# A retention and FP4 feed-forward kernel: the transposes of the normalised heads go behind the value projection, the gate projection ahead of the output projection

## The chip, the cores and the metric

The kernel runs on one core of a Trainium2 chip. The metric is the device time of one execution in microseconds; a comparison is between medians of runs. The granted clock that the profile gives for TensorE (PE) is a share of full speed, where 1.00 is 2.4 GHz and 0.50 is 1.2 GHz.

## The reference

Two sequences of 2048 tokens with 256 features each pass through a retention layer and a feed-forward layer, each with a residual and a layer norm:

```
q, k, v = split(x @ w_qkv.T);  q, k = xpos(q, k)          # 8 heads, 32 wide; v 64 wide
ret = einsum(q, k) * scale * decay ** (t - s)  (causal)
o   = einsum(ret, v);  normed = (o - mean(o)) / sqrt(var(o) + EPS)   # per head
x   = layernorm(x + (silu(x @ w_gated.T) * normed) @ w_proj.T)
xq, wq = fp4_quant_dequant(x), fp4_quant_dequant(w)       # blocks of 16
x   = layernorm(x + fp4_linear(silu(gate) * up, w_down))
```

## The kernel before

The 4096 tokens are 32 tiles of 128 tokens; the tiles alternate between the two sequences, so a tile's state depends on that of the tile two before. Tile n is worked on in "body n". Every engine has its own hand-written `body(n, b, piece)`, with b = n % 2, and runs its instructions in that order; semaphores tie the engines together. Bodies 8 to 29 are in a hardware loop over pairs of tiles; those before and behind are written out. The feed-forward stage (`ffn_body`) follows for all tiles. Most products are made of three float32r products (high by high, high by low, low by high), so each needs a high and a low copy of its input.

TensorE's body n before the change, in order (n+1 is the next tile, n-3 an older one, since `LAG` is 3):

1. `turn_qk(n)` (L1396): four transposes of the rotated queries and keys into the PSUM bank `turn`.
2. `project_qk(n+1)` (L1362), a product of six 512-column matmuls.
3. `scores(n)` (L1410), which waits for ScalarE's `copy_qkT(n)` (L433) and `open_gate(n)` (L443), and for VectorE's `add_resid` (L681) of tile n-4.
4. `turn_gated(n-3)` (L1459): four transposes of the gated, normalised heads into `turn`. It waits for `gated_ready` of tile n-3 and for VectorE's `decay_q(n)` (L666), which reads the same bank.
5. `update(n)` (L1446) and `cross(n)` (L1421), the new state's product and the product with the carried state; `cross` waits for `decay_q(n)`.
6. `project_v(n+1)` (L1362). It writes `proj[:, 1]`, one of the four banks in which the scores lie, and so waits for `ret_ready` of tile n: VectorE's `decay_scores(n)` (L674), which reads all the scores.
7. `mix(n)` (L1433), the product of the decayed scores and the values.
8. `project_out(n-3)` (L1362 on `wproj`), twelve 256-column matmuls, which waits for VectorE's `split_gated(n-3)` (L1078); its result goes to `add_resid(n-3)`, `resid_stats` and `resid_moments`.
9. `project_gate(n+1)` (L1362), which waits for `ret_ready` too.

ScalarE starts its body with `copy_qkT(n)` and then `open_gate(n)`; further down come `copy_gatedT(n-3)` (L413, out of `turn`), `place_state` (L477), `copy_v(n+1)` (L438) and `square_heads(n)` (L448). VectorE has `decay_q`, `decay_scores`, short steps of the quantisers and of the inverse square roots, `split_gated`, then `rotate_products` and `rotate_sum` (L647 to L659) of tile n+1, on which the next `turn_qk` waits; then `apply_gate` (L691), `add_resid`, `resid_stats`, `sum_squares` (L698), and in even bodies `x_max` (L781). Bodies 0 to 2 have no `turn_gated` and no `project_out`, because there is no tile n-3. In body 31 there is no tile n+1, and weight transposes of the feed-forward layer (`turn_weights`) stand ahead of and behind `mix`.

Of the kernel before, what the change touches and what calls it, by code (L numbers as in the profile page):

```python
# [35 lines left out]
TILES = BATCH * CHUNKS  # L36
# [37 lines left out]
LAG = 3  # L74
# [16 lines left out]
def retention_ffn(nc, x_tok, x_feat, w_in, w_proj, w_gu, w_down, decay, tables, eye, pow_dram, out):  # L91
    with ExitStack() as ctx:
# [196 lines left out]
        def in_turn(n):  # L289

            return valid(n) and valid(n + LAG)
# [108 lines left out]
        def _(act):  # L400
# [9 lines left out]
            def copy_gatedT(n):  # L410
                act.wait_ge(gated_turned, n + 1)
                need(act, y_done, n)
                act.activation(gatedT_hi[:], turn[:], ACT.Copy).then_inc(gatedT_ready, 1)  # L413
# [6 lines left out]
            def round_w_from(piece):  # L420
                act.wait_ge(w_fp4["step"], FP4_STEPS * (piece + 1))
                part = w_fp4["rounder"][:, 0]
                act.activation(part, part, ACT.Copy, bias=ROUNDER_FROM, scale=ROUNDER_BY).then_inc(w_fp4["rounder_ready"], 1)
# [56 lines left out]
            def body(n, b, piece):  # L480
                if valid(n):
                    copy_qkT(n)
                if valid(n):
                    open_gate(n, b)
                if valid(n + 2) and not (isinstance(n, int) and n < 0):
                    split_x(n + 2, b)
                low, high = range(PER), range(PER, HEADS)
                if valid(n - 2) and b == 1:
                    normalise_half(n - 2, b, low)
                if in_turn(n - LAG):  # L490
                    copy_gatedT(n - LAG)
                if valid(n - 2) and b == 1 and not weights(n, 0):
                    normalise_half(n - 2, b, high)
                if piece is not None and b == 1:
                    round_w_from(piece)
                for group in weights(n, 0):
                    turn_weights(group)
                if carried(n - 1):
                    place_state(n - 1, 1 - b)
                if valid(n + 1):  # L500
                    copy_v(n + 1, 1 - b)
                if isinstance(n, int) and n == 0:
                    act.wait_ge(ld_proj, 32)
                    act.activation(wproj_hi[:], wproj, ACT.Copy).then_inc(wproj_hi_ready, 1)
                if valid(n - 2) and b == 0:
                    normalise_half(n - 2, b, low)
                if valid(n):
                    square_heads(n)
                if valid(n - 2) and b == 0:
                    normalise_half(n - 2, b, high)  # L510
                if b == 1 and tiles_of(n - 1) and not (isinstance(n, int) and n == TILES - 1):
                    round_x_from(n - 1)
                for group in weights(n, 1):
                    turn_weights(group)
                if weights(n, 1):
                    split_xq(0, 0)
                    normalise_half(n - 2, b, high)
                if b == 0 and tiles_of(n):
                    norm_x1(n)
# [102 lines left out]
        def _(dve):  # L622
# [38 lines left out]
            def decay_q(n):  # L661
                dve.wait_ge(qkT_ready, n + 1)
                if isinstance(n, int) and n == 0:
                    dve.wait_ge(ld_dq, 16 * PER)
                need(dve, out_done, n)
                dve.tensor_tensor(qdT[:].rearrange("p g t -> p (g t)"), turn[:, 0:GROUPS * P],  # L666
                                  dq[:].rearrange("p g t -> p (g t)"), ALU.mult).then_inc(qd_ready, 1)

# [23 lines left out]
                                  gate[:, b].rearrange("p (g r c) -> p r g c", g=GROUPS, r=2), ALU.mult).then_inc(opened_ready, 1)  # L692

            def sum_squares(n, b):
                need(dve, resid_stats_done, n - LAG + 1)
                need(dve, joint_ready, n - b)
                dve.wait_ge(squared, n + 1)
                dve.tensor_reduce(moments[:, b, 2:2 + HEADS], head_cols(squares[:]), AX.X, ALU.add).then_inc(heads_summed, 1)  # L698
# [159 lines left out]

            def body(n, b, piece):
                joint, x, w = b == 0 and valid(n - 2), b == 1 and bool(tiles_of(n - 1)), piece is not None  # L860
                if joint:
                    joint_var(n)
                    joint_guess(n)
                if valid(n):
                    decay_q(n)
                if valid(n):
                    decay_scores(n)
                if x:
# [12 lines left out]
                if w and b == 1:  # L881
                    w_unit(piece)
                    w_exponent(piece)
                if in_turn(n - LAG):
                    split_gated(n - LAG)
                if joint:
                    joint_fine(n)
                for group in weights(n, 0):
# [7 lines left out]
                if x and not (isinstance(n, int) and n == TILES - 1):  # L896
                    x_unit(n - 1)
                    x_exponent(n - 1)
                if valid(n + 1):
                    rotate_products(n + 1, 1 - b)  # L900
                    rotate_sum(n + 1, 1 - b)
# [5 lines left out]
                    turn_weights(group)  # L907
                if weights(n, 1):
                    split_xq(0, 0)
                if in_turn(n - LAG):  # L910
                    add_resid(n - LAG, 1 - b)
                    resid_stats(n - LAG, 1 - b)
                if valid(n):
                    sum_squares(n, b)
                if in_turn(n - LAG):
                    resid_moments(n - LAG, b)
                if b == 0 and tiles_of(n):
                    x_max(n)
                if isinstance(n, int) and n == -1:
# [307 lines left out]

            def finish(n):
                if n == 0:
                    joint_chain(TILES)  # L1230
                    split_gated(TILES - LAG)

# [125 lines left out]
        def _(pe):  # L1358
# [115 lines left out]
            def body(n, b, piece):  # L1474
                if valid(n):
                    turn_qk(n, b)
                if valid(n + 1):
                    project_qk(n + 1, 1 - b)
                if valid(n):
                    scores(n)  # L1480
                if in_turn(n - LAG):
                    turn_gated(n - LAG, 1 - b)
                if carried(n):
                    update(n, b)
                if valid(n):
                    cross(n, b)
                for group in weights(n, 0):
                    turn_weights(group)
                if valid(n + 1):
                    project_v(n + 1, 1 - b)  # L1490
                if isinstance(n, int) and n == -1:
                    flip_mask()
                if valid(n):
                    mix(n, b)
                for group in weights(n, 1):
                    turn_weights(group)
                if isinstance(n, int) and n == TILES - 1:
                    turn_xq(0, 0)
                if in_turn(n - LAG):
                    project_out(n - LAG)  # L1500
                if valid(n + 1):
                    project_gate(n + 1, 1 - b)

            def flip_mask():

# [136 lines left out]
```

## Time and profile before

| what | us |
|---|---|
| median of 3 runs | 589.22 |
| lowest, highest | 589.04, 592.42 |
| the profiled execution | 590.8 |
| its span | 589.0 |
| TensorE busy in it | 565.3 |
| VectorE busy in it | 513.6 |

TensorE's matmul ends are modelled, so its busy time hides short waits. Starts are measured: the distance from the start of one group of weight loads (PEld) to the next says how long a step of TensorE lasted, waiting included. "issue" behind a row names idle time for which the trace has no releaser.

### The profile page before, as it was taken

To read this page: it belongs to the slowest core of one execution; us is meant where nothing else is said; L and a number is where in the kernel's file an instruction comes from. 1 tells how busy PE (TensorE), PEld (TensorE's weight loads), DVE (VectorE), ACT (ScalarE), POOL (GpSimd) and SP (SyncE) were. 2 spreads that over 40 slices of the span, in tenths; PEclk is the share of its full clock that TensorE was granted. 3 is DMA by queue.
4 is the path that set the end of the run, shared out by engine and by line. 5 is a ranking of instruction groups with operands and counts; after the bars stand their busy time and mean duration, and the time that the engine had idled before them with its cause. 6 is when DMAs were issued, how large, how long until landed. Compare 5 with 4: busy or idle time off the path is not lost.

```text
span 589.0 us, 14053 instructions
## 1 busy us (share of the span) xinstructions
PE 565.3 (96%) x4432; PEld 486.4 (83%) x4432; DVE 513.6 (87%) x1283; ACT 338.0 (57%) x818; POOL 228.3 (39%) x260
## 2 busy tenths in 40 slices
PE   6999999999999999999999879999999999999983
PEld 3778888888888888888888768889999999999973
DVE  6567878988998998899899858999999999888896
ACT  3446766766676676667667634435444545445442
POOL 2211121435334343533434213554655645554420
PEclk9999999999999999999999979999999999999997
DMA  6601210210111011001101000000010101000002
GB/s 206 219 20 46 55 46 12 55 53 18 36 53 45 9 53 53 26 28 53 45 9 45 11 9 11 0 1 2 1 37 1 37 1 37 18 20 19 19 18 90
DMA packets 24983, 22.32 MB, mean 38 GB/s; under 512 B 2025, under 2 KB 21874, under 8 KB 24946
## 3 DMA queue, kind: packets, MB, share of 16 engines
q1 hardware_dynamic: 24130, 20.27, 11.6%
q10 hardware_dynamic: 816, 1.57, 0.9%
q8 instruction: 21, 0.34, 0.3%
q14 instruction: 16, 0.13, 0.1%
HBM read 17.63 MB, written 4.20 MB: 37 GB/s over the span
## 4 chain that ended last, share of the span: by engine, by line
PE 86%; DVE 7%; DMA 2%; issue 2%; POOL 2%; ACT 1%; ACTq 0%; DVEq 0%; POOLq 0%
PE wide_banks L1362 58%; PE wide_banks L1433 9%; PE wide_banks L1410 4%; PE wide_banks L1421 3%; PE wide_banks L1550 3%; PE turn L1459 3%; PE turn L1396 2%; PE wide_banks L1446 2%; DVE shared L852 1%; DVE shared L857 1%; DVE shared L674 1%; PE turn L1559 1%; DMA pow_dram<-powers 1%; DMA wgu_lo<-pow_dram 1%; POOL shared L1323 1%
## 5 line engine op out<-in xcount | busy, mean ns | idle before, releaser
L1328 POOL TENSOR_TENSOR shared<-shared,h_scale 128x704 f32<-128x704 bf16 x31 | 43.0, 1388 | 78.7 <-DVE shared L857 78.7
L1362 PE MATMUL wide_banks<-win_hi,x_hi 128*128 128x512 f32 x192 | 66.5, 428 | 2.6 <-DVE shared L674 1.5
L461 ACT ACTIVATE shared<-opened,rstd 128x64 f32<-128x64 f32 x240 | 63.6, 340 | 2.2 <-DVE rstd L770 2.1
L1433 PEld LDWEIGHTS wide_banks<-shared 128*128 128x128 f32 x512 | 62.0, 192 | 2.8
L1362 PE MATMUL wide_banks<-wgu_hi,xq_hi 128*128 128x512 f32 (+1 forms) x192 | 60.7, 397 | 3.4 <-DVE xq_lo L1065 3.4
L556 ACT ACTIVATE shared<-wide_banks 128x512 f32<-128x512 f32 x64 | 29.6, 462 | 58.0 <-PE wide_banks L1362 57.5
L1433 PE MATMUL wide_banks<-shared 128*128 128x64 f32 x512 | 60.6, 271 | 0.0
L1362 PE MATMUL wide_banks<-win_hi,x_lo 128*128 128x512 f32 x192 | 60.4, 396 | 0.0
L1362 PE MATMUL wide_banks<-win_lo,x_hi 128*128 128x512 f32 x192 | 60.3, 395 | 0.0
L1362 PE MATMUL wide_banks<-wgu_lo,xq_hi 128*128 128x512 f32 (+1 forms) x192 | 57.4, 380 | 0.0
L1362 PE MATMUL wide_banks<-wgu_hi,xq_lo 128*128 128x512 f32 (+1 forms) x192 | 57.0, 379 | 0.0
L427 ACT ACTIVATE shared<-shared 128x704 bf16<-128x704 f32 x32 | 25.3, 791 | 54.0 <-POOL shared L1323 51.6
L1323 POOL TENSOR_TENSOR shared<-shared,h_inv 128x704 f32<-128x704 f32 x31 | 43.2, 1392 | 26.7 <-DVE h_inv L848 26.7
L674 DVE TENSOR_TENSOR shared<-wide_banks,shared 128x1024 f32<-128x1024 f32 x32 | 39.2, 1225 | 14.4 <-PE wide_banks L1410 14.4
L1279 POOL TENSOR_TENSOR x_lo<-xf,x_hi 128x256 fp32r<-128x256 f32 x32 | 23.3, 728 | 70.9 <-DVE qdT L666 42.9
L433 ACT ACTIVATE qkT<-turn 128x512 f32<-128x512 f32 x32 | 19.2, 599 | 42.9 <-PE turn L1396 42.9
L1362 PEld LDWEIGHTS wide_banks<-win_hi,x_lo 128*128 128x128 f32 x192 | 36.1, 188 | 8.7
L1362 PEld LDWEIGHTS wide_banks<-win_lo,x_hi 128*128 128x128 f32 x192 | 36.2, 189 | 8.2
L1362 PEld LDWEIGHTS wide_banks<-wgu_hi,xq_lo 128*128 128x128 f32 x192 | 36.1, 191 | 6.1
L1362 PEld LDWEIGHTS wide_banks<-wgu_lo,xq_hi 128*128 128x128 f32 x192 | 36.1, 191 | 6.0
L1269 POOL TENSOR_TENSOR x_unit<-x_unit,x_rounder 128x512 f32<-128x512 f32 (+1 forms) x17 | 20.8, 1225 | 50.7 <-DVE shift L775 46.8
L1245 POOL TENSOR_TENSOR kd<-shared 128x128 f32<-128x128 f32 x60 | 23.2, 407 | 38.6 <-DVE shared L659 34.4
(146 smaller groups left out, 1438.9 us busy)
## 6 DMA issues: line engine op xcount, KB each, us to landing
xf<-in_x_feat SPq DMA_DIRECT2D x32, 128.0 KB, 2.2
tab<-in_tables SPq DMA_DIRECT2D x16, 256.0 KB, 2.7
xt<-in_x_tok SPq DMA_DIRECT2D x32, 128.0 KB, 2.1
out<-x SPq DMA_DIRECT2D x32, 128.0 KB, 1.7
x<-in_w_in ACTq DMA_DIRECT2D x3, 512.0 KB, 5.8
w<-in_w_gu SPq DMA_DIRECT2D x1, 1408.0 KB, 8.0
w<-in_w_down SPq DMA_DIRECT2D x1, 704.0 KB, 9.3
wgu_lo<-pow_dram SPq DMA_DIRECT2D x1, 576.0 KB, 4.5
```

What stands on the lines that cost most here:

```text
L427: act.activation(h_size[:, b], h_unit[:, b], ACT.Abs, scale=SIZE_BY).then_inc(h_fp4["rounder_ready"], 1)
L461: last = act.activation(gated[:, b, cols], opened[:, b, cols], ACT.Copy, scale=rstd[:, b, 1 + k:2 + k])
L556: act.activation(silu[:, cols[0]:cols[1]], proj[:, part, 0:cols[1] - cols[0]], ACT.Silu).then_inc(silu_done[part], 1)
L674: dve.tensor_tensor(ret[:].rearrange("p (j g) t -> p j (g t)", g=GROUPS), row_scores, dmask[:].rearrange("p (j g) t -> p j (g t)", g=GROUP ...
L1245: last = pool.tensor_tensor(kd[:, P * g:P * (g + 1)].rearrange("p (j d) -> p j d", d=DQ), rot[:, b, QK + P * g:QK + P * (g + 1)].rearrange ...
L1269: pool.tensor_tensor(unit, unit, rounder, ALU.add).then_inc(x_fp4["rounded"], 2)
L1279: pool.tensor_tensor(x_lo[:, b], xf[:, b], x_hi[:, b].bitcast(F32), ALU.subtract).then_inc(x_lo_ready, 1)
L1323: pool.tensor_tensor(over_blocks(h_unit[:, b]), over_blocks(h[:, b]), spread(h_fp4["inv"][:]), ALU.mult).then_inc(h_fp4["step"], 1)
L1328: pool.tensor_tensor(over_blocks(hq[:, b]), over_blocks(h_steps[:, b]), spread(h_fp4["scale"][:, b]), ALU.mult).then_inc(h_fp4["ready"], 1)
L1362: last = pe.matmul(dst, lhs, rhs, start=k == 0, stop=k == len(parts) - 1)
L1410: last = pe.matmul(row_scores[:, j, P * g:P * (g + 1)], qkT[rows, GROUPS + g], qkT[rows, g], start=True, stop=True)
L1433: last = pe.matmul(mixed[:, r, DV * at:DV * (at + 1)], ret[:, slot(k)], vs[:, b, DV * k:DV * (k + 1)], start=False, stop=k >= HEADS - 2, s ...
```

## The change

TensorE: `turn_gated(n-3)` goes from behind `scores(n)` to behind `project_v(n+1)`, directly ahead of `mix(n)`; `project_gate(n+1)` goes ahead of `project_out(n-3)`. ScalarE: `copy_gatedT` goes behind `copy_v`, `round_w_from` behind that. VectorE: `decay_q` opens the body; `resid_moments` goes from the end of a body into the next one, behind `decay_q`; `split_gated` goes behind `x_unit` and `x_exponent`, directly ahead of `rotate_products`; `sum_squares` goes ahead of `add_resid`. A wait of `sum_squares` on the residual's statistics goes to `decay_q`, for a tile one older. The last `resid_moments` is in `finish(0)`.

```diff
 # TensorE
                 if valid(n):
                     scores(n)
-                if in_turn(n - LAG):
-                    turn_gated(n - LAG, 1 - b)
                 if carried(n):
                     update(n, b)
 ...
                     project_v(n + 1, 1 - b)
                 if isinstance(n, int) and n == -1:
                     flip_mask()
+                if in_turn(n - LAG):
+                    turn_gated(n - LAG, 1 - b)
                 if valid(n):
                     mix(n, b)
 ...
+                if valid(n + 1):
+                    project_gate(n + 1, 1 - b)
                 if in_turn(n - LAG):
                     project_out(n - LAG)
-                if valid(n + 1):
-                    project_gate(n + 1, 1 - b)
 # ScalarE
-                if in_turn(n - LAG):
-                    copy_gatedT(n - LAG)
 ...
-                if piece is not None and b == 1:
-                    round_w_from(piece)
 ...
                     copy_v(n + 1, 1 - b)
+                if in_turn(n - LAG):
+                    copy_gatedT(n - LAG)
 ...
+                if piece is not None and b == 1:
+                    round_w_from(piece)
 # VectorE
+                need(dve, resid_stats_done, n - LAG)          # in decay_q
 ...
-                need(dve, resid_stats_done, n - LAG + 1)      # in sum_squares
 ...
+                if valid(n):
+                    decay_q(n)
+                if valid(n) and valid(n - 1 - LAG):
+                    resid_moments(n - 1 - LAG, 1 - b)
                 if joint:
                     joint_var(n)
                     joint_guess(n)
-                if valid(n):
-                    decay_q(n)
 ...
-                if in_turn(n - LAG):
-                    split_gated(n - LAG)
 ...
+                if in_turn(n - LAG):
+                    split_gated(n - LAG)
                 if valid(n + 1):
                     rotate_products(n + 1, 1 - b)
 ...
+                if valid(n):
+                    sum_squares(n, b)
                 if in_turn(n - LAG):
                     add_resid(n - LAG, 1 - b)
                     resid_stats(n - LAG, 1 - b)
-                if valid(n):
-                    sum_squares(n, b)
-                if in_turn(n - LAG):
-                    resid_moments(n - LAG, b)
 # VectorE, finish(0)
+                    dve.wait_ge(resid_stats_done, TILES - LAG)
+                    resid_moments(TILES - 1 - LAG, 1)
```

## Rows read from the trace of the kernel before

**Rows 1.** Page: TensorE's busy time, and its granted clock in 40 slices.
```profile
PE 565.3 (96%) x4432; PEld 486.4 (83%) x4432; DVE 513.6 (87%) x1283; ACT 338.0 (57%) x818; POOL 228.3 (39%) x260
...
PEclk9999999999999999999999979999999999999997
```

**Rows 2.** Timeline (start, us, engine, line, what), one looped tile: TensorE's weight loads.
```profile
200.16 0.54 PEld L1410 LDWEIGHTS wide_banks<-qkT 32*128 32x128 f32 x16 [0.36 <-issue]
...
200.82 0.42 PEld L1459 LDWEIGHTS turn<-ident,shared 128*128 128x128 f32 x4
...
201.41 0.27 PEld L1446 LDWEIGHTS wide_banks<-shared,kd 128*32 128x32 f32 x16 [0.17 <-issue]
...
201.77 0.52 PEld L1421 LDWEIGHTS wide_banks<-shared,qdT 64*128 64x128 f32 x8
...
202.41 0.30 PEld L1362 LDWEIGHTS wide_banks<-win_hi,x_hi 128*128 128x128 f32 x2
...
203.69 1.98 PEld L1433 LDWEIGHTS wide_banks<-shared 128*128 128x128 f32 x16
...
205.59 0.54 PEld L1362 LDWEIGHTS wide_banks<-wproj_hi,gatedT_hi 128*128 128x128 f32 x4
...
207.01 0.31 PEld L1362 LDWEIGHTS wide_banks<-win_hi,x_hi 128*128 128x128 f32 x2
...
208.28 0.59 PEld L1396 LDWEIGHTS turn<-ident,shared 128*128 128x128 f32 x4
...
210.45 0.54 PEld L1410 LDWEIGHTS wide_banks<-qkT 32*128 32x128 f32 x16 [0.37 <-issue]
```

**Rows 3.** Timeline, the same tile: what VectorE and ScalarE do around the scores.
```profile
200.96 1.23 DVE L674 TENSOR_TENSOR shared<-wide_banks,shared 128x1024 f32<-128x1024 f32 x1 [0.25 <-PE wide_banks L1410]
...
209.16 0.60 ACT L433 ACTIVATE qkT<-turn 128x512 f32<-128x512 f32 x1 [0.76 <-PE turn L1396]
...
209.65 0.59 ACT L443 ACTIVATE shared<-wide_banks 128x512 f32<-128x512 f32 x1
```

**Rows 4.** Timeline, tile 2, which has no turned heads and no output product.
```profile
37.05 0.57 PEld L1410 LDWEIGHTS wide_banks<-qkT 32*128 32x128 f32 x16 [0.38 <-issue]
...
37.74 0.27 PEld L1446 LDWEIGHTS wide_banks<-shared,kd 128*32 128x32 f32 x16
37.87 1.23 DVE L674 TENSOR_TENSOR shared<-wide_banks,shared 128x1024 f32<-128x1024 f32 x1 [1.07 <-PE wide_banks L1410]
38.10 0.52 PEld L1421 LDWEIGHTS wide_banks<-shared,qdT 64*128 64x128 f32 x8
...
39.21 0.30 PEld L1362 LDWEIGHTS wide_banks<-win_hi,x_hi 128*128 128x128 f32 x2 [0.58 <-issue]
...
39.24 0.70 PE L1362 MATMUL wide_banks<-win_hi,x_hi 128*128 128x512 f32 x2 [0.42 <-DVE shared L674]
...
40.48 1.99 PEld L1433 LDWEIGHTS wide_banks<-shared 128*128 128x128 f32 x16
...
45.84 0.56 PEld L1410 LDWEIGHTS wide_banks<-qkT 32*128 32x128 f32 x16 [0.38 <-issue]
```

**Rows 5.** Timeline, the looped tile again: ScalarE's and VectorE's rows near the moved steps.
```profile
204.11 0.60 ACT L438 ACTIVATE shared<-wide_banks 128x512 f32<-128x512 f32 x1 [0.78 <-PE wide_banks L1362]
...
205.24 0.69 DVE L647 TENSOR_TENSOR qk_cos<-wide_banks,tab 128x512 f32<-128x512 f32 x1
...
206.97 0.41 DVE L659 TENSOR_TENSOR shared<-qk_cos,wide_banks 128x256 f32<-128x256 f32 x1
...
210.54 0.41 DVE L666 TENSOR_TENSOR qdT<-turn,dq 128x256 f32<-128x256 f32 x1
```

**Rows 6.** Timeline at the change of stages, and busy time by stretch (PE, PEld, DVE, ACT, POOL, PEclk, DMA, GB/s).
```profile
345.08 1.22 PE L1362 MATMUL wide_banks<-wgu_hi,xq_hi 128*128 128x512 f32 x2 [3.20 <-DVE xq_lo L1065]
...
345.00:350.00 5.00, 4.92 (x14) 3.97 (x15) 4.39 (x16) 1.19 (x2) 1.25 (x2) 0.50 0.09 26
```

## The prediction

> **What bounds the kernel now.** I read the page first. TensorE is busy for 565.3 of 589.0 us, at a granted clock of nine tenths or more in all slices but two [rows 1]. Busy time of TensorE can't show a short wait, so I went to the timeline and took the distances between the starts of its groups of weight loads. In the loop one tile takes 210.45 - 200.16 = 10.29 us [rows 2] (all 26 distances from tile 4 to tile 30 are 10.28 to 10.30), made up so: scores 0.66, turned heads 0.59, state product 0.36, cross product 0.64, value projection 1.28, mix 1.90, output product 1.42, gate projection 1.27, and 2.17 from the start of `turn_qk` to the next scores [rows 2].
>
> Two links in this chain go over another engine. The first is that last 2.17 us: transposes, ScalarE's copy of them (209.16 to 209.76) and its gate (to 210.24), then scores at 210.45, 0.21 behind the gate's end [rows 2, 3]. The query and key projection in between is six 512-column matmuls, 1.28 us like its sister, and 2.17 - 0.57 (the transposes) - 1.28 leaves about 0.3 us of waiting. The second runs from scores over VectorE's `decay_scores` to `project_v`: the decay starts 0.80 us behind the scores' start and takes 1.23 [rows 3], so it ends at 202.19, and the value projection starts at 202.41 [rows 2]. TensorE's own work between the two, 0.66 + 0.59 + 0.36 + 0.64 = 2.25 us, just covers this link. The turned heads are 0.59 of that cover.
>
> **What the cover is worth: tiles 0 to 2.** Bodies 0 to 2 have no turned heads, so they already have TensorE's order of the changed kernel between scores and `project_v`. In tile 2 [rows 4] the scores start at 37.05, the state product follows 0.69 later, the cross product at 1.05, and the value projection at 39.21, which is 2.16 behind the scores. Its weight load has 0.58 us of idle time ahead of it and its first matmul 0.42 us, put down to `decay_scores`, which ran from 37.87 to 39.10. Tiles 0 and 1 show the same 2.14 and 2.16. So the link over VectorE takes 2.16 us with nothing but 1.7 us of work inside it, and 2.25 us with the turned heads inside: the four transposes cost 2.25 - 2.16 = 0.09 us where they stand.
>
> **The change part by part.**
>
> *Turned heads behind `project_v`.* In the new place nothing waits beside them: the engine runs value projection, transposes, mix in sequence. Their price there is a transpose group between full products. `turn_qk`, the same four transposes, takes 0.57 us in such a place, 0.59 in the old one with its 0.17 of issue [rows 2]. So each tile gives back 0.09 and pays 0.57: +0.48, or +0.50 with 0.59. A gain is excluded by the 2.16 of rows 4, unless `decay_scores` itself gets shorter or starts earlier, and it starts 0.80 (before) and 0.82 (tile 2) behind the scores, released by TensorE both times [rows 3, 4]. The least it can cost is 0, if the 0.58 of idle time in tiles 0 to 2 had a cause of its own; the most is 0.59 + 0.09 = 0.68, if the transposes also break up the pipelining of their new neighbours as much as they gain now. I take 0.50.
>
> *Gate projection ahead of the output product.* Both keep their 1.27 and 1.42 us [rows 2]. Could the gate now be opened earlier, which would shorten the 0.3 us wait ahead of scores? ScalarE still has `copy_qkT` ahead of `open_gate` in its queue, and starts it only at 209.16 when the transposes are done; the gate projection had ended before that even in the old order [rows 2, 3]. So 0. The swap hides the heads' new path: transposes at 3.43 behind the scores (2.16 + 1.27), ScalarE's copy behind `copy_v`. `copy_v` starts 1.70 behind its projection's start (202.41 to 204.11) [rows 2, 5], so at 3.86, and the copy of the heads ends at about 3.86 + 0.5 + 0.6 = 4.96; VectorE's `split_gated` ends near 5.7. Mix starts at 4.00, gate at 5.90, output product at 7.17: 1.5 us of slack. Without the swap it would be 0.2.
>
> *VectorE's order.* `split_gated` now stands directly ahead of the rotations. In even bodies they start at 5.08 now [rows 5] (205.24 - 200.16) and at about 5.65 then, and the rotated keys are ready near 7.8 rather than 7.22 (207.38). The next `turn_qk` stands at 7.17 + 1.42 = 8.59, so 0.6 us is left after the 0.2 of a release. Behind them: amax of a weight piece, gate, squares' sum, residual (near 9.4 to 9.8; scores at 10.79 waits for it), statistics, `x_max`, and `decay_q` of the next body at about 10.83, which is 0.05 behind the next scores; now it is at 0.09 (210.54 to 210.45) [rows 2, 5]. Then `resid_moments`, and VectorE is free for `decay_scores` about 0.6 behind the scores, with 0.80 wanted. The cover there is 0.2 us, in every second tile. `cross` waits for `decay_q`, ends 0.45 behind the scores, wanted at 1.02. I cost all of this at 0. GpSimd, which gets the rotated keys about 0.6 us later, has till the next state product, 0.66 behind the next scores, so 3.6 us for 0.8 of work.
>
> **Sum.** New period: 2.16 + 1.27 + 0.58 + 1.90 + 1.27 + 1.42 + 2.17 = 10.77 to 10.79. It can be checked from the other side: tile 2's period is 8.79 [rows 4], and with output product and transposes added it is 8.79 + 1.42 + 0.57 = 10.78. From scores 3 to scores 31 are 28 periods, 28 x 0.50 = 14.0. In body 31 weight transposes take `project_v`'s place and wait for the same decay; the turned heads come behind them and push all that follows by 0.59. 14.0 + 0.6 = 14.6 us. The span becomes 589.0 + 14.6 = 603.6, the profiled execution 590.8 + 14.6 = 605.4, and the median 589.22 + 14.6 = 603.8.
>
> *The clock.* In tiles 0 to 2 TensorE waits 0.42 us in the matmul row of each tile, and slices 2 and 3 of the page, from 14.7 us on, stand at nine tenths or more [rows 1, 4]. So waits of 0.5 us per tile left the clock at its full level. The Trainium skill, "Perfetto Trace Analysis", section Matmul Optimizations, says that the matmul engine scales its power with its use and that matmuls should therefore run back to back. That rule speaks against this change; the trace, with 0.42 us per tile at the full clock, doesn't show it for waits of this size. By the rule the sum would be more than 14.6; by the rows it is 14.6.
>
> **Rivals.**
>
> A. *The transposes are free in the new place (not slower).* Place: the start of `project_v`. If the 0.58 us of idle time in tiles 0 to 2 came from something that the loop doesn't have, `project_v` would follow the cross product at 0.66 + 0.36 + 0.64 = 1.66, and the 0.59 taken away there would pay for the 0.59 added: 589.2 us. It decides from the point at which `decay_scores` ends less than 1.5 us behind the scores' start. Against it: its end at 2.03 in both rows [rows 3, 4]. 5%.
>
> B. *The gate comes early.* If the wait ahead of scores hung on the gate projection and not on ScalarE's order, up to 0.33 us per tile would go: 29 x 0.33 = 9.6, so 603.8 - 9.6 = 594.2. Against it: ScalarE's gate starts directly behind the copy [rows 3]. 4%.
>
> C. *VectorE becomes late for `decay_scores`.* If its row in even bodies is 0.5 us longer than I count, the 0.2 of cover is gone and each second tile loses 0.3: 14 x 0.3 = 4.2, so 608.0. For it: VectorE's row from the rotations on has no gap. 13%.
>
> D. *The half clock at the change of stages.* Behind a 3.20 us wait of TensorE the clock stands at 0.50 in 345 to 350 [rows 6]; with its edges (0.91 in the 5 us on either side) it is some 6.8 us at half speed, which cost about 3.1 us of the work that ran in it from 345.08 on. If this doesn't happen in the changed kernel, 603.8 - 3.1 = 600.7; if it happens once more, 606.9. For it: one of three runs before was 3.2 us longer. 13%.
>
> E. *Half clock in the loop,* the rule above. If the clock fell for such a stretch once in the stage, it would be 606.9, and if in every other tile, 14 x 3.1 = 43 us more, 647. Against it: rows 1 and 4. 1%.
>
> **Numbers.** The forecast itself has 64%: 603.8 us, with its own bounds 0.40 and 0.60 per tile, so 601 to 607. C and both halves of D lie inside 599.5 to 608.5, A, B and E's far end outside, and that leaves out no more than 2 in 10 with the outer parts of C and D. A difference of over 1% (5.9 us) is about what a measurement of this kernel tells from no change. Slower by over 1%: the forecast, C, D and E, 0.90 after a share for what I don't see. Within 1%: A and B, 0.07. Faster: 0.03, since no rival worked out here reaches it.
>
> **What would show it.** Right, if the looped period is 10.78 us; `project_v` starts 2.15 to 2.17 behind scores, with an idle time of about 0.58 before its weights and 0.42 before its matmul, put down to L674, in all tiles; the transposes (L1459) take 0.57 between `project_v` and mix; scores still follow ScalarE's gate by 0.2. Wrong, if `project_v` starts at 1.7 (A), if scores start less than 2.1 behind `turn_qk` (B), or if L674 starts later than 0.8 behind the scores in every second tile (C).

## The result, and the profile after

| | median of runs, us | runs | ratio to before, 95% interval |
|---|---|---|---|
| before | 590.17 | 4 | |
| after | 603.00 (601.25 to 605.43) | 4 | 1.0214 (1.0185 to 1.0244) |

The change makes the kernel about 12.8 us slower. The profiled execution of after has a span of 601.9 us, 12.9 more than before's. It splits so, by the start of the scores of tile 3 and of tile 31: up to tile 3 1.45 us (45.84 to 47.29), the 28 periods from tile 3 to tile 31 10.77 us (287.86 to 298.63), and what follows 0.68 us (255.30 to 255.98).

The page of after (busy time; TensorE's clock in 40 slices):

```profile
PE 566.8 (94%) x4432; PEld 490.2 (81%) x4432; DVE 515.9 (86%) x1283; ACT 336.0 (56%) x818; POOL 228.3 (38%) x260
...
PEclk9999999999999999999999989999999999999998
```

TensorE's busy time has grown by 1.5 us against [rows 1]; all the rest of the 12.9 is new idle time. The waits of after's TensorE (us in total, times, longest):

```profile
PE wide_banks L1364 <- DVE shared L675: 14.7, 31, 0.8
```

L675 is `decay_scores`, L1364 the wide product. Before had four such waits, 1.5 us in all. One looped tile of after in the timeline, from its `turn_qk` (tile 19, an odd one), to be laid beside [rows 2, 4]:

```profile
215.90 0.47 PEld L1398 LDWEIGHTS turn<-ident,shared 128*128 128x128 f32 x4
216.00 0.60 PE L1398 MATMUL turn<-ident,shared 128*128 128x128 f32 x4
...
217.93 0.54 PEld L1412 LDWEIGHTS wide_banks<-qkT 32*128 32x128 f32 x16 [0.36 <-issue]
217.93 0.73 PE L1412 MATMUL wide_banks<-qkT 32*128 32x128 f32 x16
...
218.59 0.27 PEld L1448 LDWEIGHTS wide_banks<-shared,kd 128*32 128x32 f32 x16
...
218.72 1.22 DVE L675 TENSOR_TENSOR shared<-wide_banks,shared 128x1024 f32<-128x1024 f32 x1 [0.25 <-PE wide_banks L1412]
218.95 0.52 PEld L1423 LDWEIGHTS wide_banks<-shared,qdT 64*128 64x128 f32 x8
...
220.06 0.30 PEld L1364 LDWEIGHTS wide_banks<-win_hi,x_hi 128*128 128x128 f32 x2 [0.59 <-issue]
220.09 0.70 PE L1364 MATMUL wide_banks<-win_hi,x_hi 128*128 128x512 f32 x2 [0.43 <-DVE shared L675]
...
221.34 0.60 PEld L1461 LDWEIGHTS turn<-ident,shared 128*128 128x128 f32 x4
...
221.57 0.60 PE L1461 MATMUL turn<-ident,shared 128*128 128x128 f32 x4
...
221.90 1.87 PEld L1435 LDWEIGHTS wide_banks<-shared 128*128 128x128 f32 x16
222.01 1.90 PE L1435 MATMUL wide_banks<-shared 128*128 128x64 f32 x16
...
223.69 0.30 PEld L1364 LDWEIGHTS wide_banks<-win_hi,x_hi 128*128 128x128 f32 x2
223.72 0.72 PE L1364 MATMUL wide_banks<-win_hi,x_hi 128*128 128x512 f32 x2
...
224.97 0.66 PEld L1364 LDWEIGHTS wide_banks<-wproj_hi,gatedT_hi 128*128 128x128 f32 x4
```

The 0.43 us of idle time ahead of the value projection is tile 2's picture of [rows 4], now in every tile. The slots, from start to start of weight loads, in us:

| slot | before [rows 2] | after | difference |
|---|---|---|---|
| scores to value projection | 2.25 | 2.13 | -0.12 |
| value projection | 1.28 | 1.28 | 0 |
| turned heads in the new place | | 0.56 | +0.56 |
| mix | 1.90 | 1.79 | -0.11 |
| gate projection | 1.27 | 1.28 | +0.01 |
| output product | 1.42 | 1.56 | +0.14 |
| `turn_qk` to scores | 2.17 | 2.03 | -0.14 |
| one tile | 10.29 | 10.63 | +0.34 |

Odd tiles of the loop take 10.63 us, even ones 10.72; the mean over tiles 9 to 28 is 10.68 against 10.28.

Four of these differences (0.56, -0.11, 0.14, -0.14) are partly a matter of where the ruler is laid. The first weight load of a group starts some way ahead of its first matmul, and this lead differs: the transposes' load stands 0.23 us ahead behind 512-column matmuls (221.34 to 221.57) and 0.10 ahead behind 256-column ones (215.90 to 216.00), that of mix 0.11 ahead behind the transposes. From the start of one group's matmuls to the next, the turned heads take 222.01 - 221.57 = 0.44 us and mix 1.71, as in before (1.70). From `turn_qk` to the scores it is 217.93 - 216.00 = 1.93 us, and in before 1.93 too:

```profile
208.52 0.60 PE L1396 MATMUL turn<-ident,shared 128*128 128x128 f32 x4
...
210.45 0.73 PE L1410 MATMUL wide_banks<-qkT 32*128 32x128 f32 x16
```

### The profile page after: what moved, and what is told of

Read it like the earlier page. It is cut to its first block and busy times, and to the rows that moved or that the text cites. A ratio compares the mean times of both kernels' runs of the same rounds, so it can differ in the third digit from the quotient of the medians.

```text
span 601.9 us, 14053 instructions
## 1 busy us (share of the span) xinstructions
PE 566.8 (94%) x4432; PEld 490.2 (81%) x4432; DVE 515.9 (86%) x1283; ACT 336.0 (56%) x818; POOL 228.3 (38%) x260
## 5 line engine op out<-in xcount | busy, mean ns | idle before, releaser
L1364 PE MATMUL wide_banks<-win_hi,x_hi 128*128 128x512 f32 x192 | 68.8, 439 | 14.9 <-DVE shared L675 14.7
L1364 PE MATMUL wide_banks<-wgu_hi,xq_hi 128*128 128x512 f32 (+1 forms) x192 | 60.2, 395 | 3.4 <-DVE xq_lo L1065 3.4
L461 ACT ACTIVATE shared<-opened,rstd 128x64 f32<-128x64 f32 x240 | 62.1, 340 | 0.4
L556 ACT ACTIVATE shared<-wide_banks 128x512 f32<-128x512 f32 x64 | 29.6, 462 | 57.0 <-PE wide_banks L1364 56.5
L1435 PEld LDWEIGHTS wide_banks<-shared 128*128 128x128 f32 x512 | 60.6, 194 | 0.3
L1364 PE MATMUL wide_banks<-win_lo,x_hi 128*128 128x512 f32 x192 | 60.4, 396 | 0.0
L1364 PE MATMUL wide_banks<-win_hi,x_lo 128*128 128x512 f32 x192 | 60.3, 395 | 0.0
L1364 PE MATMUL wide_banks<-wgu_lo,xq_hi 128*128 128x512 f32 (+1 forms) x192 | 57.0, 378 | 0.0
L1364 PE MATMUL wide_banks<-wgu_hi,xq_lo 128*128 128x512 f32 (+1 forms) x192 | 56.8, 377 | 0.0
L438 ACT ACTIVATE shared<-wide_banks 128x512 f32<-128x512 f32 x32 | 19.1, 597 | 58.3 <-PE wide_banks L1364 58.3
L675 DVE TENSOR_TENSOR shared<-wide_banks,shared 128x1024 f32<-128x1024 f32 x32 | 39.0, 1220 | 9.3 <-PE wide_banks L1412 9.3
L1364 PEld LDWEIGHTS wide_banks<-win_hi,x_hi 128*128 128x128 f32 x192 | 29.2, 191 | 21.8 <-issue 21.7
L1364 PEld LDWEIGHTS wide_banks<-win_hi,x_lo 128*128 128x128 f32 x192 | 36.1, 188 | 8.7
L1364 PEld LDWEIGHTS wide_banks<-win_lo,x_hi 128*128 128x128 f32 x192 | 36.1, 188 | 8.7
L1364 PEld LDWEIGHTS wide_banks<-wgu_hi,xq_lo 128*128 128x128 f32 x192 | 35.8, 189 | 6.0
```

Source lines behind the costliest of these rows:

```text
L438: act.activation(vs[:, b], proj[:, 1], ACT.Copy).then_inc(v_copied, 1)
L461: last = act.activation(gated[:, b, cols], opened[:, b, cols], ACT.Copy, scale=rstd[:, b, 1 + k:2 + k])
L556: act.activation(silu[:, cols[0]:cols[1]], proj[:, part, 0:cols[1] - cols[0]], ACT.Silu).then_inc(silu_done[part], 1)
L675: dve.tensor_tensor(ret[:].rearrange("p (j g) t -> p j (g t)", g=GROUPS), row_scores, dmask[:].rearrange("p (j g) t -> p j (g t)", g=GROUP ...
L1364: last = pe.matmul(dst, lhs, rhs, start=k == 0, stop=k == len(parts) - 1)
L1435: last = pe.matmul(mixed[:, r, DV * at:DV * (at + 1)], ret[:, slot(k)], vs[:, b, DV * k:DV * (k + 1)], start=False, stop=k >= HEADS - 2, s ...
```

## Experiments

Theory 1: the four transposes were TensorE's cover for the way from the scores over VectorE's `decay_scores` to the value projection, and cost their own time in the new place. Theory 2: the loss comes from the new orders of VectorE and ScalarE, or from the swap of the two products. Periods below are those of the loop in the profiled run of each kernel.

**The decay in two parts.** The value projection overwrites one of the four banks that the decay reads. This kernel is after, with that bank decayed first and the value projection waiting for it alone (the code is shortened).

```diff
+ for rows, done in ((slice(0, 1), ret0_ready), (slice(1, PER), ret_ready)):
+     dve.tensor_tensor(ret[rows], row_scores[:, rows], dmask[rows], ALU.mult).then_inc(done, 1)
 # project_v
-                need(pe, ret_ready, n)
+                need(pe, ret0_ready, n)
```

> The changed kernel with decay_scores cut in two: the bank that project_v overwrites first (a quarter of the columns), then the other three; project_v waits for the first alone. Theory 1: first part about 0.4 us, so it ends near 1.2 behind scores' start, and project_v starts at 1.66 to 1.7 (behind cross, no wait), not at 2.14: period 10.67 - 0.47 = about 10.2 us, and the time falls by 12 to 13 us to about that of the kernel before. Theory 2: only the extra instruction on VectorE is seen, 0.1 to 0.2 us a tile, and the time stays at after's or above (+13 to +18 against before).

586.15 us, ratio to before 0.9944 (0.9913 to 0.9975), some 2.6% below after by the two ratios. Its timeline, tile 19:

```profile
207.65 0.54 PEld L1414 LDWEIGHTS wide_banks<-qkT 32*128 32x128 f32 x16 [0.36 <-issue]
...
208.45 1.29 DVE L677 TENSOR_TENSOR shared<-wide_banks,shared 128x256 f32<-128x256 f32 x2 [0.24 <-PE wide_banks L1414]
208.67 0.52 PEld L1425 LDWEIGHTS wide_banks<-shared,qdT 64*128 64x128 f32 x8
...
209.31 0.30 PEld L1366 LDWEIGHTS wide_banks<-win_hi,x_hi 128*128 128x128 f32 x2
```

The value projection starts 1.66 us behind the scores, with no idle time, and odd tiles take 10.15 us, 0.48 less than in after. Both numbers are those that theory 1 gave. Even tiles take 10.28, because the decay starts later there (see `joint_guess` below). The 28 periods are 13.4 us shorter than in after, as expected; the time fell by some 16 us (by the two ratios) and not by 12 to 13. Tiles 0 to 2 won another 1.4 us (8.30 to 8.33 each, from 8.76 to 8.80), and in the profiled run the clock stood at 1.00 from 330 to 360 us, behind the loop, where after's and before's fell for a while. Taking away this one wait gives back more than the whole loss, with all new orders in place.

**The same cut in the kernel before.** The same edit as above, on before.

> The kernel before with the decay cut in two as in the changed one. Theory 1: the way over VectorE is just covered there by TensorE's 2.25 us, so the cut can give at most the small rest: project_v at 2.25 still, period 10.28 (10.17 at best, as for a wait of 0.1 us), time 0 to 3 us below before; that it gives 15 us in the changed kernel and next to none here is what shows that the turned heads were the cover. Rival: if it gives 10 us or more here too, the cut helps in another way and the split run says nothing about the change.

588.68 us, 0.9985 (0.9972 to 0.9998): 0.9 us at the most likely. The value projection stays at 2.25 behind the scores in odd tiles, the period at 10.28; even tiles are 10.32 to 10.36, and only tiles 0 to 2, which have no turned heads, go from 8.77 to 8.79 down to 8.32 to 8.39. Where the transposes stand in the way the loop has nothing to win; where they are gone the same cut is worth 2.7% of before's time, some 16 us.

**Three of four transposes left out, in before and in after; and all four done twice, in after.** Each of the three ran once, so they are read by their periods.

```diff
-                for c in range(VC):                 # turn_gated, tiles 0 to 28
+                for c in range(1):                  # left out
+                for c in list(range(VC)) * 2:       # twice
```

> The kernel before with only the first of the four transposes of the gated heads in tiles 0 to 28; three are left out, as in the other run. Cover theory: their room between scores and project_v is nearly free, since project_v can't start before 2.14 to 2.16 behind scores anyway: project_v moves from 2.25 to 2.14, the period from 10.28 to 10.17, 3 us in all, with an idle time of 0.2 to 0.3 us ahead of it. Rival: if transposes cost TensorE their own time in either place, the period falls by 0.33 here too, 9 us in all.

> The changed kernel with only the first of the four transposes of the gated heads in the loop's tiles (0 to 28); the other three are left out, so three quarters of the turned heads are wrong there. Price of a transpose in the new place: TensorE's clean rate would be 0.11 us each, so the turned heads' slot shrinks by 0.33 us and so does the period: 10.63 to 10.30 in odd tiles, 9 to 10 us less in all. If the new place were free (rival A): no change of the period.

> The changed kernel with the four transposes done twice in tiles 0 to 28 (the result is the same). Four more at the clean rate of 0.11 us: 0.44 to 0.47 us per tile, period 11.07 to 11.10 in odd tiles, 12 to 13 us more than after. If the prediction's 0.57 for four transposes was right and only something else made after's period shorter: 0.57 per tile, 16 us more.

Before's period falls to 10.16 to 10.21, most often 10.17 or 10.18, so about 0.11 us for three transposes. Its span is 584.5, 4.5 less, of which 2.85 are in the 28 periods. The value projection now starts at 2.14 with idle time ahead of it:

```profile
210.75 0.30 PEld L1362 LDWEIGHTS wide_banks<-win_hi,x_hi 128*128 128x128 f32 x2 [0.34 <-issue]
```

In after the odd period falls to 10.31, so 0.32 us for the same three. The even one falls only from 10.72 to 10.52, by 0.20: `decay_scores` starts 1.02 us behind the scores there, and the value projection 2.34. The 28 periods are 7.6 us shorter, the span is 592.9, 9.0 less. Twice four raise the odd period to 11.07 and the even one to 11.16, by 0.44 each, the 28 periods by 12.3 us and the span to 613.2, 11.3 more. A transpose in the new place costs 0.11 us, four cost 0.44. With 0.57 for four, as predicted, the last run would have had 11.20. Here are its matmuls: eight transposes from 227.44, mix from 228.31, so 0.87 us for eight.

```profile
227.44 1.03 PE L1461 MATMUL turn<-ident,shared 128*128 128x128 f32 x8
...
228.31 1.90 PE L1435 MATMUL wide_banks<-shared 128*128 128x64 f32 x16
```

**After, with the output product first again.**

```diff
-                if valid(n + 1):
-                    project_gate(n + 1, 1 - b)
                 if in_turn(n - LAG):
                     project_out(n - LAG)
+                if valid(n + 1):
+                    project_gate(n + 1, 1 - b)
```

> The changed kernel with the output product ahead of the gate projection again; the turned heads stay behind the value projection. Theory 1: turn_qk follows 512-column matmuls again, so turn_qk to scores is 2.17 and not 2.03 us, and the output product now stands 0.1 to 0.2 us behind split_gated's end: period 10.63 + 0.14 + up to 0.1 = 10.77 to 10.9, time 4 to 7 us above after. If the swap gives nothing: same as after (+13 against before).

601.37 us, 1.0183 (1.0146 to 1.0220); the interval overlaps that of after. `turn_qk` to scores is 2.16 again, but the odd period stays at 10.63 (the even one is 10.67): the output product takes 1.42 and not 1.56. So the 0.14 us that the swap seems to win at one seam it pays at the other. It is the lead of the transposes' weight load, 0.24 us behind 512-column matmuls (208.28 in [rows 2] to 208.52) and 0.10 behind 256-column ones, and no time. The expectation was wrong to take it for a gain.

**After, with the turned heads back behind the scores.**

```diff
                 if valid(n):
                     scores(n)
+                if in_turn(n - LAG):
+                    turn_gated(n - LAG, 1 - b)
```

> The changed kernel with its turned heads back behind scores; the gate projection stays ahead of the output product, and VectorE's and ScalarE's new orders stay. Theory 1 (the four transposes were TensorE's cover for the way over VectorE's decay_scores, and the rest of the change is harmless): value projection 2.25 us behind scores again, the shorter 2.03 us from turn_qk to scores stays, so the loop's period is 10.28 - 0.14 = 10.14 us, and the kernel is about 29 x 0.14 = 4 us faster than the one before (ratio 0.993). Theory 2 (the loss came from the new orders on VectorE and ScalarE): the period stays near 10.6 to 10.7 and the time some 12 us above before.

595.83 us, 1.0097 (1.0069 to 1.0124): half of the loss is gone, and the expected gain didn't come. Periods are 10.45 in even and 10.63 in odd tiles. The expected 10.14 was out of reach anyway, since its 0.14 is the seam just told; against 10.28 the new orders and the swap together cost 0.17 and 0.35 here. TensorE's waits name another place (first line), and the timeline around tile 19 shows it:

```profile
PE turn L1461 <- DVE qdT L667: 3.1, 11, 0.3
```

```profile
208.08 0.69 DVE L1078 TENSOR_TENSOR gatedT_lo<-turn,gatedT_hi 128x512 fp32r<-128x512 f32 x1 [0.81 <-ACT gatedT_hi L413]
...
213.31 0.54 PEld L1412 LDWEIGHTS wide_banks<-qkT 32*128 32x128 f32 x16 [0.37 <-issue]
...
213.77 0.41 DVE L667 TENSOR_TENSOR qdT<-turn,dq 128x256 f32<-128x256 f32 x1
...
214.33 0.63 PE L1461 MATMUL turn<-ident,shared 128*128 128x128 f32 x4 [0.29 <-DVE qdT L667]
```

`decay_q` runs 0.46 behind the scores and not at 0.09 as in [rows 5]: VectorE has waited 0.81 us for ScalarE's late copy ahead of `split_gated`, and from there to `decay_q` its row has no gap. The transposes overwrite what `decay_q` reads, and wait. In even tiles another step is late: `decay_scores` starts 1.07 us behind the scores and the value projection 2.40.

**TensorE as before, ScalarE and VectorE as after.** The last two edits together.

> TensorE in the order of before, ScalarE and VectorE in the order of after. Theory 1 as it stands after turned-heads-back: VectorE's row is too long with split_gated directly ahead of the rotations, behind ScalarE's copy of v: turn_gated has to wait for decay_q in odd tiles. With the output product first again the residual comes 1.3 us earlier, so part of that goes: period 10.3 to 10.5, time 0 to 5 us above before. If the new orders cost nothing: the time of before. If the 12 us of the change were theirs: 12 us above.

600.92 us, 1.0191 (1.0168 to 1.0213): worse than expected, as slow as after, by another wait. The waits of TensorE, and the timeline:

```profile
PE wide_banks L1364 <- DVE gatedT_lo L1078: 5.6, 29, 0.8
```

```profile
221.33 0.69 DVE L1078 TENSOR_TENSOR gatedT_lo<-turn,gatedT_hi 128x512 fp32r<-128x512 f32 x1
...
222.07 0.53 PEld L1364 LDWEIGHTS wide_banks<-wproj_hi,gatedT_hi 128*128 128x128 f32 x4 [0.31 <-DVE gatedT_lo L1078]
```

Mix to output product is 2.29 us and not 1.90. Theory 2 is thus true of this combination. In after itself the output product stands 7.04 us behind the scores, behind turned heads and gate projection, and not 5.43, so `split_gated`, which ends at 5.72, holds nothing up. There the orders cost next to nothing in odd tiles: before's 10.28, less the turned heads' 0.59 in the old place, plus 0.44 in the new one is 10.13, and the split decay has 10.15. No run moves the turned heads alone in before, so what the orders do without the move, and the move without the orders, isn't separated fully.

**Before, with the gate projection first.**

> The kernel before with one edit: gate projection ahead of the output product. If the 0.14 us that turn_qk to scores became shorter comes from this swap alone: period 10.14 us, 4 us faster than before (0.993). Against it: VectorE keeps add_resid ahead of sum_squares here, and the output product's end is later by 1.27 us, so add_resid would start 1.0 to 1.3 us later and VectorE's row up to decay_scores could be late: then the period is 10.3 or more and the gain is gone.

602.86 us, 1.0200 (1.0174 to 1.0226). The rival in the expectation was right, and worse than put: the period is 10.73 to 10.81.

```profile
PE turn L1459 <- DVE qdT L666: 10.6, 27, 0.5
```

```profile
214.92 0.42 DVE L681 TENSOR_TENSOR resid<-wide_banks,xt 128x256 f32<-128x256 f32 x1 [0.47 <-PE wide_banks L1362]
...
216.47 0.54 PEld L1410 LDWEIGHTS wide_banks<-qkT 32*128 32x128 f32 x16 [0.36 <-issue]
...
217.10 0.41 DVE L666 TENSOR_TENSOR qdT<-turn,dq 128x256 f32<-128x256 f32 x1
...
217.63 0.42 PEld L1459 LDWEIGHTS turn<-ident,shared 128*128 128x128 f32 x4 [0.63 <-issue]
```

VectorE waits 0.47 us for the output product, everything behind it slides, `decay_q` comes 0.63 behind the scores, and the turned heads behind that. The change puts `sum_squares` (0.69 us) ahead of `add_resid`, and in after's tile 19 `add_resid` has no wait; no run tests that step by itself.

**`joint_guess` late.** In even tiles of after, `decay_scores` starts 0.90 behind the scores and not 0.79. The timeline of tile 18, whose scores start at 207.22:

```profile
207.43 0.74 POOL L1281 TENSOR_TENSOR x_lo<-xf,x_hi 128x256 fp32r<-128x256 f32 x1 [1.43 <-ACT x_hi L408]
207.61 0.59 DVE L734 TENSOR_SCALAR root<-var 128x18 int32<-128x18 int32 x1
...
208.12 1.21 DVE L675 TENSOR_TENSOR shared<-wide_banks,shared 128x1024 f32<-128x1024 f32 x1
```

`joint_guess` (L734) took 0.18 us in before each time, 16 of 16. Here it takes 0.59, and ends (208.20) as GpSimd's `x_lo` does (208.17). In tile 30, where there is no `x_lo` any more, it takes 0.18 again. This agrees with the Trainium skill, "SBUF — State Buffer", section Who interferes with whom: a `tensor_scalar` can use the port pair that VectorE shares with GpSimd, and whichever comes second waits for the whole instruction of the first. Here `x_lo` starts at 207.43 and `joint_guess` at 207.61. The experiment, on after:

```diff
-                if joint:
-                    joint_var(n)
-                    joint_guess(n)
                 if valid(n):
                     decay_scores(n)
+                if joint:
+                    joint_var(n)
+                    joint_guess(n)
```

> The changed kernel with joint_var and joint_guess behind decay_scores. Theory 1: even tiles lose the 0.09 us by which they are longer than odd ones (10.72 against 10.63), 11 x 0.09 = 1 us in all, and joint_guess takes 0.18 us again, since no GpSimd instruction runs beside it there (or stays at 0.59 if that is its own); the rest of the 12 us stays. If VectorE's row is what costs the 12 us: more than 3 us are won.

600.23 us, 1.0170 (1.0147 to 1.0192). Even and odd tiles both take 10.63 to 10.64, and the step is short again:

```profile
207.77 0.17 DVE L734 TENSOR_SCALAR root<-var 128x18 int32<-128x18 int32 x1
```

So 0.09 us of each even tile in the loop, 0.8 us over the 28 periods (298.63 to 297.85), was VectorE being late for the decay. The ratio itself doesn't tell this from after.

**The split decay with the late `joint_guess`.** Both edits on after.

> The split decay once more, and VectorE's joint_var and joint_guess behind decay_scores in even bodies. In the first split run decay_scores started 1.26 behind scores in even tiles (0.80 in odd ones) behind a joint_guess that took 0.59 instead of 0.18 us. Theory 1 (VectorE's row ahead of the decay is the next limit, by those 0.46 us): the decay starts at 0.80 to 0.85 in even tiles too, periods 10.15 in all, so 11 x 0.13 = 1.4 us faster than the first split run, 5 us below before (0.991). If the 0.41 us of joint_guess only go elsewhere in VectorE's row and that row is itself the limit: no faster than the first split run (0.994).

587.77 us, 0.9956 (0.9937 to 0.9975). From tile 4 to tile 29 the periods are 10.15 or 10.16, as expected, and the 28 periods take 283.96 us, 1.3 less than in the first split run. The time doesn't show it: what comes after tile 31's scores takes 257.25 us and not 254.23. In this run TensorE stood at half clock for a part of that stage (granted 0.66, 0.59 and 0.73 in the 5 us from 330, 340 and 345 on), and the first split run had 1.00 there throughout. The gain of the loop is real, and smaller than this scatter.

**And `open_gate` ahead of `copy_qkT` on ScalarE.**

```diff
+                if valid(n):
+                    open_gate(n, b)
                 if valid(n):
                     copy_qkT(n)
-                if valid(n):
-                    open_gate(n, b)
```

> The version with the split decay and the late joint_guess, and on ScalarE open_gate(n) ahead of copy_qkT(n). This is the prediction's rival B in the form in which it could work: with the gate projection ahead of the output product the gate's input is ready 1.5 us before the turned queries and keys. Theory: scores then follow the copy of the turned queries and keys by 0.2, and TensorE's own 0.56 + 1.28 us become the limit between turn_qk and scores: 1.84 to 1.9 us and not 2.03, period 9.96 to 10.05, so 28 x 0.1 to 0.19 = 3 to 5 us below split_guess_late (ratio to before 0.987 to 0.991). Rival: VectorE's row, free for the decay at 0.68 behind scores in odd tiles, is the limit at once (decay later than 0.80, project_v later than 1.66): less than 2 us.

584.68 us, 0.9892 (0.9870 to 0.9913), the fastest version. But the expected mechanism failed: the period is 10.15 to 10.16 as without the edit, and that the ratio fell into the expected 0.987 to 0.991 is luck. Tile 19 and tile 31 of this kernel (the latter has no query and key projection behind `turn_qk`):

```profile
206.40 0.58 ACT L444 ACTIVATE shared<-wide_banks 128x512 f32<-128x512 f32 x1
...
207.29 0.60 ACT L434 ACTIVATE qkT<-turn 128x512 f32<-128x512 f32 x1 [0.30 <-PE turn L1400]
...
208.03 0.63 PE L1366 MATMUL wide_banks<-win_hi,x_lo 128*128 128x512 f32 x2
...
208.58 0.54 PEld L1414 LDWEIGHTS wide_banks<-qkT 32*128 32x128 f32 x16 [0.36 <-issue]
```

```profile
328.80 0.60 ACT L434 ACTIVATE qkT<-turn 128x512 f32<-128x512 f32 x1 [0.30 <-PE turn L1400]
...
329.45 0.54 PEld L1414 LDWEIGHTS wide_banks<-qkT 32*128 32x128 f32 x16 [0.92 <-ACT qkT L434]
```

With the gate done at 206.98 and the copy at 207.89, scores still start at 208.58. In tile 31 they start 0.05 us behind the copy and 1.39 behind `turn_qk`. So in the loop neither copy nor gate is waited for. What stands ahead of the scores is the projection itself: its last two 512-column matmuls start at 208.03 and, by the profile, run past 208.58. The 0.36 us is idle time of the weight loads alone: the scores' first load starts with its matmul and not ahead of it. From those two matmuls' start to the scores is 0.55 us, where the two 512-column matmuls ahead of them took 0.47 (207.56 to 208.03), so some 0.1 us a tile is lost there at most.

The margin over the version above lies outside the loop. 0.6 us is the period of tile 30 (9.18 against 9.80): without a projection in between, tile 31's scores do follow the gate or the copy, whichever is last, and there the edit works. The rest is for the most part the clock in the stage after: at the same mean granted clock the spans of the two versions are 583.1 against 583.3 and 583.8 us (0.991), and 585.3 against 585.8 to 586.6 (0.986).

## Why the prediction was right, and where it was off

603.8 us was predicted and 603.0 measured. The agreement to 0.8 us is in part luck: the cost was put at 14.6 us and is 12.8, and the median of before, with a fourth run, is 590.17 and not the 589.22 from which the forecast was added up. Step by step:

- **The cover** was right. `project_v` starts 2.13 to 2.14 behind the scores in odd tiles, with 0.59 idle before its weights and 0.43 before its matmul, put down to L675; 2.15 to 2.17, 0.58 and 0.42 were given. The split decay and the left-out transposes show it twice over: three transposes are worth 0.11 us in the old place and 0.32 in the new (odd tiles).
- **The price per tile** is the term that was mis-sized: 0.50 predicted, 0.34 in odd and 0.43 in even tiles measured. The sum took the 0.57 of `turn_qk` as a cost. That is the distance between starts of weight loads, and the first load of a group leads its matmul by more behind 512-column matmuls (0.23 us) than behind 128-column ones (0.11). The new slot is 0.56, but mix behind it shrinks from 1.90 to 1.79, which the sum left at 1.90. Four transposes cost 0.44, by the starts of their matmuls and by doing them twice. With it and the measured give-back of 0.12 (2.25 to 2.13; predicted 0.09) the sum is 0.32, and the odd tiles' 0.34 is nearly met.
- **The swap** at 0 was right, seam and all (`out_first`). Without it the slack was to be 0.2 us. In `out_first` it is 0.05 (`split_gated` ends 5.73 us behind the scores, the product's weights start at 5.78), no more than where the product waits (222.02 to 222.07 in the run with the orders alone); it cost nothing that the period shows.
- **VectorE's order** at 0 was nearly right. Rival C, VectorE late for `decay_scores` in every second tile, did come true, at 0.09 us and not 0.3, and for another reason than a miscounted row: one short step grew from 0.18 to 0.59.
- **"About 0.3 us of waiting" ahead of scores** was a wrong reading. Some 0.24 us of it is the lead of weight loads, which `turn_qk` has and the scores have not; at most about 0.1 is lost. It changed no number of the forecast. But with copy and gate both ready 0.69 us or more ahead the loop won nothing, so rival B's 594.2 us was not to be had by any order of ScalarE.
- **The signs.** The period of 10.78 did not come, and two signs of being wrong did: scores 2.03 us behind `turn_qk`, less than the 2.1 set for B, and in every second tile a decay 0.90 behind the scores, later than the 0.80 set for C. The second is C, small. The first is not B: by matmul starts the distance is 1.93 before and after. A sign in starts of weight loads changes when the neighbour does.
- **The other stages.** 28 periods were to cost 14.0 us and cost 10.8; body 31 and what follows 0.6, and it was 0.68, though the stretches at half clock in that stage differ between the two runs. The 1.45 us up to tile 3 aren't the change's work: the periods of tiles 0 to 2 are those of before (8.76 to 8.80), and between 10 and 20 us this run's clock stood lower than before's 1.00:

```profile
10.00:20.00 10.00, 8.03 (x27) 4.90 (x26) 3.39 (x6) 1.28 (x4) 3.85 (x4) 0.83 0.80 238
```

- So the forecast of the total was closer than its loop term: 3.2 us too much there, of which half came back in the profiled run by the start. Of the median's 12.8 us the loop explains 10.8 and body 31 some 0.6; the remaining 1.4 us are within the scatter of either kernel (4.2 us from lowest to highest in after). Runs of equal mean clock (0.989) have spans of 588.7 and 600.5 us, 11.8 apart, close to those 11.4.
- **Rivals A, D and E.** A fell: it would have left the loop at 10.28. D: the half clock at the change of stages came in after as in before, neither gone nor doubled (granted 0.80, 0.88 and 0.78 in the three 5 us stretches from 350 on). E fell: the clock stands at nine tenths or more in all slices of the loop, with a 0.43 us wait in each tile. The Trainium skill, "Perfetto Trace Analysis", section Matmul Optimizations, ties the engine's power to its use and asks for matmuls back to back; in this trace a wait of that size shows no effect on the clock.

## What to carry to other kernels

Ahead of moving a step off a busy engine's queue, ask which way over another engine it covers, and look for a stretch (a warm-up, a first tile) in which it is absent: that stretch is the experiment, already made. If a product waits only because it overwrites a part of what another engine reads, let that part be read first; here that took 2.7% of before's time off the changed kernel, which had lost 2.1% by reordering. Price a moved step by the starts of matmuls, or by doing it twice, not by the distance between starts of weight loads, whose lead depends on the neighbours. Compare versions at equal clock before a gain of a few tenths of a per cent is put down to an edit.

## What the runs showed of the hardware

- TensorE's weight loads stand idle for 0.36 us ahead of the first 32-row load behind full-array products, in 31 tiles of before (11.4 us) and of the last version (11.3 us), in the latter with the inputs ready 0.69 us or more ahead. The load starts with its matmul, where a full-array load behind 512-column matmuls starts 0.23 to 0.24 ahead. The array itself is at work in that time; by matmul starts some 0.1 us a tile is lost at most (an estimate: 0.55 against 0.47). Behind the transposes, ahead of the 32-column loads of `update`, the idle time is 0.17.
- A `tensor_scalar` of 18 columns on VectorE took 0.59 us in place of 0.18 while a GpSimd `tensor_tensor` ran, and ended with it.
- Four 128 x 128 float32 transposes cost TensorE 0.44 us, from doing them twice and from the starts of their matmuls; the weight loads' starts gave 0.56.
